# A mixture-of-experts layer on one core: pairs of experts run two per entry on TensorE, with their down products first, and the row blocks' high and low parts loaded to another place

## The reference, cut to what matters

```python
def cond(v, q):                       # v: 128 x 64 rows of 512, q: 128 x 256
    q_emb = relu(q @ W3 + b3)
    x = (n * v + v.sum(axis=1, keepdims=True)) * q_emb[:, None, :]
    return relu(x @ W2 + b2)          # h: 8192 rows of 512

def ffn(h):
    scores = softmax(h @ gate_w.T)    # 64 experts
    w, i = top_k(scores, 6)
    # the first 64 rows (in row order) that chose expert e, its capacity
    y[e] = (silu(buf[e] @ w_gate[e]) * (buf[e] @ w_up[e])) @ w_down[e]    # 512 x 352 and 352 x 512
    routed = sum over the kept choices of y * w
    shared = (silu(h @ sw_gate) * (h @ sw_up)) @ sw_down                  # 512 x 704 and 704 x 512
    return routed + shared

out = x + ffn(cond(x, cond_1024))
```

## Time and profile before

| | |
|---|---|
| median of 3 runs | 1211.38 us (1210.7 to 1211.5) |
| the profiled execution's own time | 1210.35 us |
| its span, first to last instruction | 1208.6 us |
| TensorE busy | 1203.1 us, 100% of the span; granted clock 1.00 throughout |
| VectorE busy | 856.9 us, 71% |
| ScalarE busy | 332.5 us, 28% |
| GpSimd busy | 271.1 us, 22% |
| mean DMA traffic | 208 GB/s |

### The profile page before, as it was taken

One profiled execution on the slowest core, in us unless ns is written; L12 is line 12 of the kernel. 1 busy time (PEld: TensorE's weight loads), 2 busy tenths in 40 slices (PEclk: granted clock), 3 DMA queues, 4 the chain that ended last, 5 costly groups with the idle time before them and its releaser, 6 DMA issues.

```text
span 1208.6 us, 15900 instructions
## 1 busy us (share of the span) xinstructions
PE 1203.1 (100%) x5693; PEld 887.8 (73%) x5693; DVE 856.9 (71%) x1872; ACT 332.5 (28%) x639; POOL 271.1 (22%) x246
## 2 busy tenths in 40 slices
PE   9999999999999999999999999999999999999998
PEld 8888888888888888888866666666666666666666
DVE  8998989988888898886655555664655664655652
ACT  6454243434334353343111111110111201111111
POOL 0000000000000000000136255263453553543421
PEclk9999999999999999999999999999999999999999
DMA  9936444372642626146667988989989899899863
GB/s 226 239 90 192 97 135 118 92 185 46 186 101 86 169 75 165 49 147 201 242 227 246 327 270 282 339 276 287 329 268 320 298 305 293 291 301 301 274 149 84
DMA packets 158999, 250.91 MB, mean 208 GB/s; under 512 B 22664, under 2 KB 93704, under 8 KB 157768
## 3 DMA queue, kind: packets, MB, share of 16 engines
q1 hardware_dynamic: 142528, 222.22, 57.9%
q0 software_dynamic: 14048, 25.18, 10.4%
q10 hardware_dynamic: 2344, 2.50, 0.7%
HBM read 197.14 MB, written 61.10 MB: 214 GB/s over the span
## 4 chain that ended last, share of the span: by engine, by line
PE 95%; DVE 3%; DMA 0%; issue 0%; ACT 0%; ACTq 0%; DVEq 0%
PE bank L1545 23%; PE bank L1546 22%; PE bank L1547 22%; PE bank L1751 13%; PE bank L1766 7%; PE bank L1571 2%; PE bank L1670 1%; PE bank L1669 1%; PE bank L1607 1%; PE bank L1605 1%; PE bank L1618 1%; DMA w2s<-in_L_cond_W_dram 0%; DVE x L965 0%; DVE xpart L969 0%; DVE x L982 0%
## 5 line engine op out<-in xcount | busy, mean ns | idle before, releaser
L1545 PE MATMUL bank<-hh,gu 128*128 128x512 f32 x704 | 278.0, 395 | 0.0
L1546 PE MATMUL bank<-hl,gu 128*128 128x512 f32 x704 | 274.2, 390 | 0.0
L1547 PE MATMUL bank<-hh,gu 128*128 128x512 f32 x704 | 274.1, 389 | 0.0
L634 POOL DMA_INDIRECT hg<-table,idx_quarter x128 | 126.6, 989 | 642.5 <-DVE idx_hi L1427 592.9
L1545 PEld LDWEIGHTS bank<-hh,gu 128*128 128x128 f32 x704 | 132.1, 188 | 39.1 <-issue 12.8
L1547 PEld LDWEIGHTS bank<-hh,gu 128*128 128x128 f32 x704 | 132.1, 188 | 27.9
L1546 PEld LDWEIGHTS bank<-hl,gu 128*128 128x128 f32 x704 | 132.2, 188 | 26.2
L702 ACT ACTIVATE ah<-prod 128x512 fp32r<-128x512 f32 x96 | 60.7, 632 | 303.2 <-DVE prod L1087 293.0
L1504 DVE STREAM_TRANSPOSE eactT<-eact 32x96 f32<-32x96 f32 (+1 forms) x512 | 133.8, 261 | 7.9
L1545 PE MATMUL bank<-sdh,ah 128*128 128x512 f32 x320 | 125.9, 393 | 0.0
L1546 PE MATMUL bank<-sdl,ah 128*128 128x512 f32 x320 | 124.6, 389 | 0.0
(11 more groups left out here) (136 smaller groups left out, 1671.0 us busy)
## 6 DMA issues: line engine op xcount, KB each, us to landing
wg<-in_L_ffn_w_gate_dram SPq DMA_DIRECT2D x64, 704.0 KB
wu<-in_L_ffn_w_up_dram SPq DMA_DIRECT2D x64, 704.0 KB
wd<-in_L_ffn_w_down_dram SPq DMA_DIRECT2D x64, 512.0 KB
table<-hrow SPq DMA_DIRECT2D x64, 256.0 KB, 4.3
x<-in_x_dram SPq DMA_DIRECT2D x60, 256.0 KB, 6.9
wd<-in_L_ffn_w_down_dram SPq DMA_DIRECT2D x64, 192.0 KB
out_dram<-outst SPq DMA_DIRECT2D x35, 256.0 KB
outst<-in_x_dram SPq DMA_DIRECT2D x32, 256.0 KB, 3.7
```

What stands on the lines that cost most here:

```text
L634: nc.gpsimd.indirect_dma_start(out=hg[p % 3][:, b, :], out_offset=None, in_=quarters, in_offset=bass.IndirectOffsetOnAxis(ap=idx_quarter[: ...
L1545: nc.tensor.matmul(o, st_h, mv_h, start=first_mm, stop=False)
L1546: nc.tensor.matmul(o, st_h, mv_l, start=False, stop=False)
L1547: return nc.tensor.matmul(o, st_l, mv_h, start=False, stop=last_mm)
```

## The change

An entry ("block" m, 16 of them) now stands for two pairs: the down products of pairs 2m - 2 and 2m - 1, then gate and up products of pairs 2m and 2m + 1. The last two pairs' down products have entries of their own ("last"). The 33 entries become 18. Blocks are at least 5.2 units of `done` apart, where a down tile is one unit and a gate_up tile 12/17; before, the entries were 2.7 apart. Three "turn" entries follow each, one tile or two apart: the rows of the next two pairs, then the transposes of the odd pair's activations in two halves.

To hold two pairs at once there are two of `hgt`, `eact`, `eactT`, a second bank for gate sums and for down sums, and a second place for down weights: `wd_odd`, where `h32` lay. The next visit's h is therefore loaded over `hl` (`h_raw`), and no sooner than the visit's last gate_up tile is done; ACT issues that load now, and DVE writes the low parts over what it reads. For space, `hg` and `ysc` go from three buffers to two.

```diff
-    GU_SHARE, FIRST_EXPERTS, EXPERTS_APART, TURN_AFTER = 12 / 17, 2.0, 2.7, 0.2
+    GU_SHARE, FIRST_BLOCK, BLOCKS_APART, LAST_APART = 12 / 17, 3.0, 5.2, 2.0
...
-        wd = [late(f"wd_{e}", [P, IT, D]) for e in range(2)]
+        wd_even = [late(f"wd_even_{e}", [P, IT, D]) for e in range(2)]
         assert late.at <= down_end
         late = Place(x_at)
-        hg = [late(f"hg{r}", [P, 2 * CAP // SQ, P]) for r in range(3)]
-        hsc = [late(f"hsc{r}", [P, E]) for r in range(3)]
-        ysc = [late(f"ysc{r}", [P, D]) for r in range(3)]
-        esilu = late("esilu", [P, I])
-        eact = late("eact", [P, IT * P])
+        hg = [late(f"hg{r}", [P, 2 * CAP // SQ, P]) for r in range(2)]
+        ysc = [late(f"ysc{r}", [P, D]) for r in range(2)]
+        eact0 = late("eact0", [P, IT * P])
+        hgt0 = late("hgt0", [P, KC, P])
+        wd_odd_tail = [late(f"wd_odd_tail_{e}", [P, D]) for e in range(2)]
         assert late.at <= x_end
         late = Place(route_at)
-        hgt = late("hgt", [P, KC, P])
+        hgt1 = late("hgt1", [P, KC, P])
...
+        h_raw = Place(hl_at)("h_raw", [P, KC, CH])
+        late = Place(h32_at)
+        wd_odd = [late(f"wd_odd_{e}", [P, IT - 1, D]) for e in range(2)]
...
+                    if m < NP // 2 and not turns and done >= FIRST_BLOCK + m * BLOCKS_APART:
+                        yield "block", m, 0
+                        turns += [(m, part) for part in range(3)]
+                        m += 1
+                    elif m == NP // 2 and p < NP and not turns and \
+                            done >= FIRST_BLOCK + (m - 0.5) * BLOCKS_APART + (p - NP + 2) * LAST_APART:
+                        yield "last", p, 0
                         p += 1
-                    elif turned < p and turned < NP and n != GT - 2 and done >= FIRST_EXPERTS + (turned + TURN_AFTER) * EXPERTS_APART:
-                        yield "turn", turned, 0
-                        turned += 1
-            assert p == NP + 1 and turned == NP
+                    elif turns and (n % 2 == 0 and n < GT - 2 or n >= GT):
+                        yield ("turn",) + turns.pop(0)
...
+            for k in range(KC):
+                sp.wait_ge(hT_stored[k], 16 * ND)
+            sp.wait_ge(s.hl_ready, KC * NCH)
+            sp.wait_ge(s.xml_ready, halves(NCH - 1))
+            load_down(1)
...
+                if kind == "block":
+                    if n > 0:
+                        load_down(2 * n)
+                        load_down(2 * n + 1)
+                    for p in (2 * n + 2, 2 * n + 3):
+                        if p < NP:
+                            load_gate(p)
+                            load_up(p)
...
-                wait(pool, s.rowsT_ready, p - 2)
+                wait(pool, s.rowsT_ready, p - 1)
...
+            gather_rows(1, range(4))
+            pool.wait_ge(s.eup_filled, 1)
+            gather_rows(2, range(4))
             gather_scores(0)
-            pool.wait_ge(s.eup_filled, 1)
-            gather_rows(1, range(4))
-            pool.wait_ge(s.eactT_ready, 1)
-            gather_rows(2, range(4))
+            pool.wait_ge(s.eact_ready, 2)
+            gather_rows(3, range(4))
             gather_scores(1)
+            gather_scores(2)
             for q in range(2):
                 pool.wait_ge(out_stored[q], 32 * ND)
             pool.wait_ge(s.x_kept, 16 * ND)
             for kind, n, j in second_stage():
-                if kind == "experts":
-
-                    if n == 0:
-                        continue
-                    ahead = n + 2 if n == 1 else n + 3
-                    scatter(n - 1, 0)
-                    gather_rows(ahead, (0, 1))
-                    scatter(n - 1, 1)
-                    gather_rows(ahead, (2, 3))
-                    if n == 1:
-                        gather_scores(2)
-                        pool.wait_ge(s.eactT_ready, 2)
-                        gather_rows(4, range(4))
-                    if n + 2 < NP:
-                        gather_scores(n + 2)
+                if kind == "block":
+                    if n > 0:
+                        scatter(2 * n - 2, 0)
+                        scatter(2 * n - 2, 1)
+                        if 2 * n + 1 < NP:
+                            gather_scores(2 * n + 1)
+                        scatter(2 * n - 1, 0)
+                    gather_rows(2 * n + 4, range(4))
+                    if n > 0:
+                        scatter(2 * n - 1, 1)
+                        if 2 * n + 2 < NP:
+                            gather_scores(2 * n + 2)
+                    gather_rows(2 * n + 5, range(4))
+                if kind == "last":
+                    scatter(n, 0)
+                    scatter(n, 1)
...
+            def load_hT(u):
+
+                for k in range(KC):
+                    act.wait_ge(hT_stored[k], 16 * (u + 1))
+                act.wait_ge(s.gu_filled, GT * (ND + u))
+                act.dma_start(h_raw[:, :, :].rearrange("p k t -> p (k t)"), hT[u]).then_inc(s.h_loaded, 16)
...
-                    silu_expert(n)
+                        load_hT(n + 1 - ND)
+                if kind == "down" and j == 2 and n + 1 < 2 * ND:
+                    split_h(n + 1 - ND)
...
+                if kind == "block":
+                    silu_expert(2 * n)
+                    silu_expert(2 * n + 1)
...
-                dve.wait_ge(gathered[p % 3], 64 * (p // 3 + 1))
-                wait(dve, s.eup_filled, p)
-                nc.vector.transpose(hgt[:, :, :].rearrange("p k (b i) -> p b k i", i=SQ),
-                                    hg[p % 3][:, :, :].rearrange("p b (j k) -> p b k j", k=KC)).then_inc(s.rowsT_ready, 1)
...
+                act = eact[p % 2][:, 0:I]
+                nc.vector.tensor_tensor(act, up_bank(p)[:, 0:I], act, ALU.mult).then_inc(s.eact_ready, 1)
...
-                if p >= 3:
-                    dve.wait_ge(s.added, 16 * after_scatter[p - 3])
+                if p >= 2:
+                    dve.wait_ge(s.added, 16 * after_scatter[p - 2])
...
-                    op = nc.vector.tensor_scalar(ysc[p % 3][rows, :], bank[6][rows, :],
+                    op = nc.vector.tensor_scalar(ysc[p % 2][rows, :], bank[6 + p % 2][rows, :],
...
+                if kind == "block":
+                    if n > 0:
+                        scale_y(2 * n - 2)
+                        scale_y(2 * n - 1)
+                    product_expert(2 * n)
+                    turn_act(2 * n, (0, 1, 2, 3))
+                    product_expert(2 * n + 1)
+                if kind == "last":
+                    scale_y(n)
+                if kind == "rows":
+                    turn_rows(0)
+                    turn_rows(1)
+                if kind == "turn":
+                    if j == 0:
+                        turn_rows(2 * n + 2)
+                        turn_rows(2 * n + 3)
+                    else:
+                        turn_act(2 * n + 1, (2 * j - 2, 2 * j - 1))
+                if kind == "down":
+                    take_down(n, j)
+                    if j == 2 and n + 1 < 2 * ND:
                         for k in range(KC):
                             split_h(NCH + n + 1 - ND, k)
...
+                    wait(pe, free, p - 1 if w is wg else p)
...
-                wait(pe, s.y_ready, p)
+                wait(pe, s.y_ready, p - 1)
...
+            def experts(m):
+                if m > 0:
+                    expert_down(2 * m - 2)
+                    expert_down(2 * m - 1)
+                expert_gate_up(2 * m)
+                expert_gate_up(2 * m + 1)
```

123 lines of the change are left out of this document (51 added, 72 removed).

## The result

The changed kernel takes 1252.4 us (median of 4 runs, 1249.6 to 1254.7) where the kernel before takes 1211.1; the ratio is 1.034 (95% interval 1.0316 to 1.0364), 41 us slower. 1240 was forecast, and 1252 lies in the range of 1208 to 1262. The profiled execution is one of 1254.7 us, span 1252.7.

The account below looks back on a forecast made before the run. TensorE, 95% of the chain that ended last, was taken as the bound. Fewer entries (-5.3), the second stage's start (+2.4) and waits for additions (+32) sum to +29 us: 1240 us, range 1208 to 1262.

Parts of the forecast that it names:

- TensorE's waits: Up products in second blocks behind an add_out wait, through DVE's scaling, for additions to free ysc: 32 us in all.
- the sum of +29: Whole kernel: -5.3 us for fewer entries, +2.4 at the second stage's start, +32 of waits ahead of up products.
- -5.3: TensorE's second stage: 33 entries become 18, saving 15 times 0.35 us of going in and out, 5.3 us less.
- The price: POOL's serial additions: 7.4 us each behind an add_out, 7.15 over the late stretch; an add_out 17.1 us.
- the prediction's own count: Block-by-block timing of additions against DVE's scaling: waits of 32 us at 7.4 us per addition, 51 at 7.8.
- With three `ysc` buffers this lateness costs nothing: Kernel before, second stage: POOL's additions run late nearly all the time, yet no scaling waits for them.
- a standing 22 us: Kernel before: pair 7's first addition goes out 22 us after its scaled sums are ready.
- the chain keeping up: Rival: POOL's additions take under 6.7 us each, no scaling waits, the kernel takes 1208.5 us; chance 0.14.
- The rival of late rows: Second stage: no wait for additions, but h or gathered rows late, 1211 to 1217 us; chance 0.06.
- Start, seams, h: Second stage: 2.4 us wait at its start, 0.35 us per entry seam, no cost from loading h over hl.

Follow-up runs that it names:

- the busy wait: Changed kernel with 60 TensorE transposes into unused columns ahead of the second up product in blocks 3, 5, 10, 12 and 14: 1252.4 us.
- the spread order: Changed kernel with each pair's four gathers on POOL placed two and two between the additions: 1282.3 us with two ysc buffers, 1243.2 with three.
- all four repairs: Changed kernel with third ysc buffer, early down products of pairs 0 and 1, gathers none/two/three/three behind a block's additions, pair 1's rows turned later: 1229.8 us.

## Why the prediction was right in its number, and where it was wrong

*TensorE's waits.* Forecast 32 us in blocks 3, 5, 10, 12 and 14, measured 34.2 in six waits. Place and releaser came out as worked out, the sum partly by luck: block by block 7.6, 3.3, 9.9, 5.3 and 7.4 us stand against 5.9, 6.6, 5.0, 7.8 and 6.6, and block 8 has 0.7 against 0. With the slower clock behind the waits the five blocks took 10.2, 5.2, 12.5, 7.2 and 8.9 us longer than a block without a wait, 44.0 in all. These 10 us beyond the waits are the term that the sum of +29 had no place for, and most of what 1240 is short of 1252; with them it is -5.3 + 2.0 + 44.0 = 40.7 against 41.3 of the medians. Keeping the clock up does not win them back, as the busy wait shows.

*The price.* The four additions behind the first `add_out` take 30.7 us (701.41 to 732.12), forecast 29.7. With the five `add_out`s between pairs 3 and 27 (81.4 us, 16.3 each where 17.1 was forecast) taken off, an addition takes (452.7 - 81.4) / 48 = 7.7 us on average, where the prediction had 7.15 for the kernel before. By the prediction's own count 7.8 us would have meant 51 us of waits; the cheaper `add_out`s worked against it. The 4.34 us of an addition in the quiet stretch is nearly twice the 2.3 us that the prediction called it near to.

*The cause*, and with it the step that failed: **"With three `ysc` buffers this lateness costs nothing"** and, from it, that the missing buffer is what turns lateness into a loss. The quoted sentence holds for the kernel before, but there two buffers cost nothing either (1211.6); it is the second half that fails: in the changed kernel the third buffer gives back 9 us of 41. The lateness is not a standing 22 us that buffers can hold; in the changed kernel POOL needs 1.4 us a pair more than TensorE asks for (18.86 against 17.47), and every reader of POOL's list comes to feel it: `ysc` with two buffers, gathered rows and scores with three.

*The part left out.* The prediction counted the gathers on POOL only for when they land ("fewer gathers between" stood as a point for the chain keeping up), not as time in which no addition can be issued. Bunching them costs the kernel before 35 us, as an amount most of what the whole change costs. In the changed kernel it is shown only as a part of the cause: the spread order brings the pace from 18.69 to 18.27 with three buffers, and the intervals that issuing ends took 7.3 us on average in place of 5.5. Also left out: that TensorE asks for the additions at 17.5 us a pair and no longer at 18.04.

*The rival of late rows* was priced for a chain on time. With the third buffer it is what TensorE waits for. *Start, seams, h.* 1.95 us of wait at the start, forecast 2.4; a block from its last shared matmul ahead to the second behind takes 15.43 us, less two slots of 0.227 that is 14.98, forecast 15.0; no wait of TensorE for the load of `h_raw`, which landed in 4.8 to 10.2 us (5.7 in the middle). So without POOL's lateness the change is worth what the sum said: 1209.2 without `add_out`, forecast 1208.5 for a chain that keeps up, with the reservation that this kernel also moves 7 MB less.

*What stays open.* With all four repairs the pace is 18.41, where the kernel before has 17.97 with two or three gathers between additions. One candidate is that a block asks for the weights of two pairs in one burst, so that more additions run beside them; for dearer landings the trace gives no sign (the 29 intervals that a landing ended took 7.9 us on average here, 8.1 before). Another is that sums now come two pairs at a time, so that POOL stands idle (22.9 us for sums and 16.1 for turned rows) and later has four additions to do. A third is the closer spacing of the blocks. Loading the second pair's weights some tiles later, and blocks 5.4 units apart, would tell them apart. Neither was tried.

## What to carry to other kernels

Before giving an engine's in-order list a burstier supply, compare its pace with the pace of the engine that sets the time (here 17.97 us a pair against the 18.04 that TensorE asked for in the kernel before, 18.86 against 17.5 in the changed one): with a list this near to its limit, time added throughout is a loss, and buffers only choose who waits. Count what stands between two links of a serial chain as issue time of its engine, not only as transfers. And put a gather that waits for another engine behind the links of the chain: between them it cost 30 us here (1282.3 against 1252.4).

## What the runs showed of the hardware that was not expected

- An addition of 128 KB to memory takes 4.3 to 4.5 us from issue to the next issue with little other traffic (DMA share 0.21 at 1186 to 1191 us in the kernel before, 0.34 at 801.77 in the one with bunched gathers) and mostly 7.5 to 8.8 beside weights. In the second case two or three gathers issued in between add nothing to see (8.0 and 8.2 us on average in the kernel before, where a landing ended the interval), in the first case five set the interval (8.47 us).
- TensorE's granted clock fell to 0.50, the lower of its two levels (1.2 GHz), during an idle time of 7.6 us in block 3, and the 16 up products behind it took 801 ns a matmul (459 otherwise); with transposes in that idle time it stayed at 1.00. The time of the kernel was the same, 1252.4 us.
